# Fetching five of 202 edge pairs' source rows one row at a time from the SP and ACT queues

## The chip, the cores and the metric

One NeuronCore of a Trainium2 chip runs the whole kernel. The metric is device time in microseconds of one execution; lower is better. Three executions of the kernel before took 2658.31, 2687.99 and 2688.67 us, a median of 2687.99 us. The profiled execution took 2666.05 us.

## The reference

The kernel computes one message-passing layer of a graph network with 6250 nodes, 206250 edges (both directions of 100000 drawn edges plus a loop per node, sorted by destination) and 128 features, all in float32.

```python
h = maximum(layernorm(x), 0)
W   = silu(edge_attr @ fw1 + fb1) @ fw2 + fb2          # [206250, 128], a filter per edge
xn  = silu(h @ aw1 + ab1) @ aw2 + ab2                  # [6250, 128], a row per node
msg = W * xn[src]                                      # gather of source rows
agg = segment_sum(msg, dst, 6250)
out = x + h + silu(agg @ ow1 + ob1) @ ow2 + ob2
```

The gather `xn[src]` picks 206250 rows of 512 bytes in random order. How these rows come into on-chip memory is what the change is about.

## The kernel before

**Tiling.** The edges are cut into 202 pairs (`PAIRS`), each of 8 tiles (`L`) of 128 edges, so one pair needs 1024 rows of `xn`. Turn s of the main loop handles pair s. A start-up part computes `xn` for all nodes in seven chunks and writes it to the DRAM tensor `node_table`; SP issues these writes (L379) and then writes the residual (L386). After that SP has nothing to do until the end of the kernel, apart from reading the count of left-over edges (L359).

**Where a pair's rows come from.** There are three sources.
- 184 *main* pairs: POOL issues one indirect DMA per tile (L439), eight per pair (four for the last), into `xg`, which has room for three pairs (`XG`). Before pair i's gathers POOL waits on `msg_done` of the main pair three before it (L436), that is, until DVE has multiplied those rows.
- 6 *early* pairs at turns 36, 51, 66, 81, 96, 111: their input rows are gathered during the start-up into `e_x`, and the node network runs on them turn by turn. `e_x` keeps one pair in each of six slots; slot r is free once turn `EARLY_TURNS[r]` has multiplied its rows.
- 12 *selected* pairs at turns 26, 41, 56, ..., 191: PE fetches their rows from the on-chip copy `parts` by multiplying with one-hot columns (L1133), six or seven blocks times three matmuls in each of turns 10 to 189. They stand in `sel_rows`.

**What a turn does.** PE multiplies the filters of pair s (L1022 and L1090), then runs a job of the side networks if one is due, then the hidden layer of pair s + 2 (L1077, which signals `pe_turn`), then the sums of an earlier pair (L1142), then the selection (L1133). ACT evaluates the job's result and the hidden layer of pair s + 2 (L504). DVE makes the one-hots (L816, L818, L861), multiplies the filters with the rows (L826, which signals `msg_done`), sums them (L829), masks them (L833) and sums again. All orders are written out at build time; there is no scheduler at run time. The job's result and the hidden layer share one PSUM bank, so PE's L1077 of a turn with a job waits until ACT has taken the job's result.

**Edge features.** ACT issues the loads of `attr` (L542), four turns' worth at a time (`PART`), into one of two halves of the tile.

**Issue points the change touches.** In `pair` of the scalar block (L592) ACT does, in order: transfers, the job, `silu_hid(s + 2)`, the copy of a finished selection (L605), then `pieces`. A wait on ACT or SP holds everything behind it in that engine's program.

Of the kernel before, what the change touches and what calls it, by code (L numbers as in the profile page):

```python
# [5 lines left out]
P = 128  # L6
# [11 lines left out]
EDGE_TILES = PAIRS * L  # L18
XG = 3
SETS = 4  # L20
PART = 4
EARLY_PAIRS = 6
EPS = 1e-5

# [45 lines left out]
assert max(SEL_TURNS) < PAIRS - 3  # L70


PIECES = [(i, min(8, NODE_TILES - i)) for i in range(0, NODE_TILES, 8)]
assert len(PIECES) + 2 < SEL_FROM


EARLY_TURNS = tuple(SEL_TURNS[r] + SEL_STEP // 2 + 3 for r in range(EARLY_PAIRS))
MAIN_TURNS = [s for s in range(PAIRS) if s not in EARLY_TURNS + SEL_TURNS]
assert len(MAIN_TURNS) == PAIRS - len(EARLY_TURNS + SEL_TURNS)
MAIN_OF = {s: i for i, s in enumerate(MAIN_TURNS)}  # L80
EARLY_OF = {s: i for i, s in enumerate(EARLY_TURNS)}

# [119 lines left out]
def run(c, d=0):  # L202

    return c + (1 + AHEAD - d)
# [4 lines left out]
    return run(s + FILL)  # L209


def gnn_layer(nc, x, e_src_t, src_t, sel_src_t, dst_t, attr_t, node_wts_t, wts_t, cols_t, rows_t, out):
# [3 lines left out]
    table = nc.dram_tensor("node_table", [NODE_TILES * P, F], f32).ap()  # L216
    resid = nc.dram_tensor("residual", [NODE_TILES * P, F], f32).ap()

    def node_rows(t, first, n):
# [5 lines left out]
    with ExitStack() as ctx:  # L225
# [3 lines left out]
        def sem(name):  # L229
# [43 lines left out]
        onehot = sb("onehot", [P, OH_SETS, 2, WIN])  # L273


        e_x = sb("e_x", [P, EARLY_PAIRS * L, F])
        e_moments = sb("e_moments", [P, 4, EARLY_PAIRS * L])
        warm = sb("warm", [P, 1])
# [6 lines left out]
        part_of = sb("part_of", [P, 2])  # L285
        sel_T = hT[:, GC:2 * GC]


        spare = sb("spare", [P, max(3 * EDGE_TILES // 2 + 4 * PAIRS, SEL_MOST * GC)])
        sel_hot = spare[:, 0:SEL_MOST * GC].bitcast(bf16).rearrange("p (b k e) -> p b k e", b=2, k=SEL_MOST)  # L290
# [45 lines left out]
        attr_in = [sem("attr_in_a"), sem("attr_in_b")]  # L336
        gathered = [sem(f"gathered{s}") for s in range(XG)]
        half_gathered = [sem(f"half_gathered{i}") for i in range(2 * len(HALVED))]
        e_gathered = [sem(f"e_gathered{r}") for r in range(EARLY_PAIRS)]
        pe_turn, hid_done, oh_done, msg_done, masked, first_done, red_done, half_msg, half_first, half_masked, half_red, win_done, group_done = (  # L340
            sem(n) for n in ("pe_turn", "hid_done", "oh_done", "msg_done", "masked", "first_done", "red_done", "half_msg",
# [11 lines left out]
            sem(n) for n in ("r_din", "r_key", "r_in", "r_gat", "r_l1", "r_hid", "r_fil", "r_msg", "r_one", "r_win",  # L353
                             "r_add", "r_taken"))
        a_l1, a_mid, a_l2, a_res, a_out = (sem(n) for n in ("a_l1", "a_mid", "a_l2", "a_res", "a_out"))

        def edges_left(eng):
            eng.wait_ge(s_left, 1)
# [4 lines left out]
        @block.sync  # L363
        def _(sp):
            sp.dma_start(e_src[:, :], e_src_t).then_inc(e_src_in, 16)
            for c in range(N_CHUNKS):
                for first, g, n in transfers(c):
                    sp.dma_start(xs[:, first:first + g * n, :].rearrange("p (g t) f -> p g t f", g=g), chunk_rows(x, first, g, n))\
                        .then_inc(s_x[c], 16)
            sp.dma_start(dst_i, dst_t).then_inc(s_dst, 16)  # L370
            sp.dma_start(wts[:, :, :], wts_t).then_inc(s_wts, 16)
            sp.dma_start(src[:, :], src_t).then_inc(src_in, 16)

            sp.sem_inc(s_tab, 16 * AHEAD)
# [36 lines left out]
        def _(pool):  # L411
# [17 lines left out]
            pool.wait_ge(src_in, 16)  # L429
            pool.wait_ge(s_tab, 16 * (AHEAD + table_writes(N_CHUNKS - 1)))  # L430

            for i, s in enumerate(MAIN_TURNS):


                if i >= XG:
# [17 lines left out]
        def _(act):  # L453
# [128 lines left out]
            def pieces(s):  # L582
# [4 lines left out]
                if 0 <= s - 1 < len(PIECES):  # L587
                    first, n = PIECES[s - 1]
                    act.wait_ge(stage_in[(s - 1) % 2], ((s - 1) // 2 + 1) * 16)
                    act.copy(parts[:, 0, first:first + n, :], hs[:, (s - 1) % 2, 0:n, :]).then_inc(part_hi, 1)  # L590

            def pair(s):  # L592
                transfers_of(s)
                for a in range(FILL) if s == 0 else ():
# [5 lines left out]
                if s in SEL_LAST:  # L600
                    h = SEL_LAST[s]
                    act.wait_ge(sel_summed, h + 1)
                    if h >= 1:
                        act.wait_ge(job_taken, job_done(("turned", h - 1)))
                    act.copy(sel_T, sel_ps).then_inc(sel_copied, 1)  # L605
                pieces(s)
                if s == STD_TURN:
                    act.wait_ge(s_var, 3)
# [36 lines left out]
        def _(dve):  # L645
# [251 lines left out]
            def pair(s):  # L897
# [11 lines left out]
                if s in EARLY_OF:  # L909
                    r = EARLY_OF[s]  # L910
                    rows_of = e_x[:, r * L:(r + 1) * L, :]
                    dve.wait_ge(job_taken, job_done(("second", 2 * r + 1)))
                elif s in SEL_OF:
                    rows_of = sel_rows[:, :, :]
                    dve.wait_ge(job_taken, job_done(("turned", 2 * SEL_OF[s] + 1)))
# [342 lines left out]
```

## Time and profile before

| | us |
|---|---|
| three executions | 2658.31, 2687.99, 2688.67 |
| profiled execution | 2666.05 |
| its span, first to last instruction | 2664.0 |
| PE busy | 1967.9 (74%) |
| DVE busy | 1480.9 (56%) |
| POOL busy | 1440.4 (54%) |
| ACT busy | 359.9 (14%) |
| mean granted TensorE clock | 0.824 |

A row of the profile's group list gives the source line, the engine, the operation, output and input by name, the count, the busy time, the mean duration, and the time that the engine sat idle before these instructions with what ended it. "Releaser remote" means that the profile could not name the instruction that ended a wait. DMA issues do not count as busy; they stand under the queue names SPq, ACTq and POOLq. A matmul's start is recorded and its end is modelled. Times of a timeline are microseconds from the start of the span.

### The profile page before, as it was taken

How to read it: one execution, taken by the hardware profiler on the slowest of the kernel's cores; microseconds unless marked ns; L12 is line 12 of the kernel's file. 1: busy time of each engine (PE TensorE's matmuls, PEld its weight loads, DVE VectorE, ACT ScalarE, POOL GpSimd, SP SyncE). 2: the span in 40 equal slices, each digit the busy share in tenths (PEclk: the TensorE clock that was granted, in tenths of full speed). 3: DMA queues.
4: the chain of work that ended last, by engine and by line, in shares of the span. 5: the costliest groups of instructions: out<-in, count | busy, mean ns of one | idle time of the engine just before them, and what ended most of it. 6: DMA issues, size and time to landing. Idle time of an engine off the chain costs nothing.

```text
span 2664.0 us, 24312 instructions
## 1 busy us (share of the span) xinstructions
PE 1967.9 (74%) x9385; PEld 1145.3 (43%) x9385; DVE 1480.9 (56%) x2778; ACT 359.9 (14%) x442; POOL 1440.4 (54%) x1523
## 2 busy tenths in 40 slices
PE   3455767777788776788878788778778788787755
PEld 2243434444444444444444344435444444444433
DVE  5376455555555555566556565645555565465545
ACT  3221111111111111111101011111010111011011
POOL 5465555454454544545655654555555556555553
PEclk9766878888888988988888888878778888797876
DMA  4432221121122222212222222222212222222221
GB/s 139 155 104 72 59 60 55 53 77 55 52 64 68 62 58 64 63 57 80 62 58 72 60 76 59 60 62 76 58 58 73 63 60 79 64 61 71 61 60 48
DMA packets 76661, 181.82 MB, mean 68 GB/s; under 512 B 26816, under 2 KB 37184, under 8 KB 70144
## 3 DMA queue, kind: packets, MB, share of 16 engines
q0 software_dynamic: 48512, 99.45, 14.2%
q10 hardware_dynamic: 21648, 69.22, 7.7%
q1 hardware_dynamic: 6384, 11.58, 1.2%
q8 instruction: 75, 1.23, 0.2%
q14 instruction: 42, 0.34, 0.0%
HBM read 170.50 MB, written 9.63 MB: 68 GB/s over the span
## 4 chain that ended last, share of the span: by engine, by line
PE 56%; another core or an unknown queue 24%; issue 13%; DVE 3%; ACT 3%; DMA 0%; ACTq 0%; SPq 0%; DVEq 0%
PE banks L1133 27%; PE banks L1090 11%; PE banks L1077 9%; PE banks L1142 4%; PE banks L1022 3%; ACT hid L504 1%; DVE sums L829 1%; PE banks L1029 1%; DVE banks L833 0%; PE banks L1018 0%; DVE banks L826 0%; PE banks L1119 0%; PE banks L1013 0%; ACT hs L578 0%
## 5 line engine op out<-in xcount | busy, mean ns | idle before, releaser
L439 POOL DMA_INDIRECT xg<-node_table,src x1468 | 1393.5, 949 | 1163.2 <-DVE banks L826 724.5
L1133 PE MATMUL banks<-spare,parts 128*128 128x512 bf16 x3528 | 921.7, 412 | 117.8 <-issue 113.5
L861 DVE TENSOR_SCALAR spare<-sel_marks 128x512 bf16<-128x512 bf16 x1176 | 265.8, 295 | 826.1 <-PE banks L1077 412.5
L1133 PEld LDWEIGHTS banks<-spare,parts 128*128 128x128 bf16 x3528 | 367.0, 106 | 607.0 <-issue 302.3
L1090 PE MATMUL banks<-wts,hid 128*128 128x128 f32 x3224 | 500.1, 297 | 111.4 <-issue 110.4
L1090 PEld LDWEIGHTS banks<-wts,hid 128*128 128x128 f32 x3224 | 486.9, 213 | 176.2 <-issue 139.8
L1077 PE MATMUL banks<-attr,wts 50*128 50x512 f32 x806 | 278.9, 765 | 302.5 <-issue 79.2
L829 DVE TENSOR_REDUCE sums<-banks 128x128 f32<-128x1024 f32 (+1 forms) x408 | 493.9, 1211 | 13.6
L504 ACT ACTIVATE hid<-banks,cols 128x1024 f32<-128x1024 f32 x202 | 224.8, 1113 | 1418.9 <-remote 914.9
L826 DVE TENSOR_TENSOR banks<-banks,xg 128x1024 f32<-128x1024 f32 (+1 forms) x186 | 224.5, 1207 | 88.5 <-remote 86.1
L833 DVE TENSOR_TENSOR banks<-banks,other 128x1024 f32<-128x1024 f32 (+1 forms) x204 | 248.7, 1219 | 7.0
L1077 PEld LDWEIGHTS banks<-attr,wts 50*128 50x128 f32 x806 | 73.6, 217 | 341.2 <-issue 281.4
L1022 PE MATMUL banks<-bias_rows,ones_b 128*128 128x512 bf16 x429 | 178.6, 416 | 35.4 <-issue 20.0
L1142 PEld LDWEIGHTS banks<-onehot,sums 128*128 128x128 f32 x816 | 128.0, 223 | 175.9 <-issue 168.5
L1142 PE MATMUL banks<-onehot,sums 128*128 128x88 f32 x816 | 157.9, 326 | 14.5 <-issue 8.3
L850 DVE TENSOR_SCALAR sel_hi<-sel_src 128x512 bf16<-128x512 uint8 x24 | 10.3, 429 | 163.0 <-remote 106.5
L1022 PEld LDWEIGHTS banks<-bias_rows,ones_b 128*128 128x128 bf16 x429 | 46.3, 108 | 75.7 <-issue 38.4
L818 DVE SCALAR_TENSOR_TENSOR onehot<-iota,ends,onehot 128x88 f32<-128x88 f32 x202 | 62.7, 311 | 9.6 <-remote 2.4
L427 POOL DMA_INDIRECT e_x<-in_x,e_src x48 | 45.7, 952 | 35.0 <-DVE res L726 18.8
L816 DVE TENSOR_SCALAR onehot<-iota,ends 128x88 f32<-128x88 f32 x202 | 53.7, 266 | 0.1
L1018 PE MATMUL banks<-node_wts,mid 128*128 128x128 f32 x194 | 26.7, 288 | 16.8 <-ACT mid L478 15.2
L1007 PE MATMUL banks<-ident,hs 128*128 128x128 f32 x97 | 16.6, 308 | 25.2 <-ACT hs L471 22.6
(109 smaller groups left out, 485.0 us busy)
## 6 DMA issues: line engine op xcount, KB each, us to landing
attr<-in_attr ACTq DMA_DIRECT2D x50, 1024.0 KB
xg<-node_table,src POOLq DMA_INDIRECT x1468
sel_src<-in_sel_src ACTq DMA_DIRECT2D x24, 256.0 KB
hs<-node_table ACTq DMA_DIRECT2D x6, 512.0 KB
resid_s<-residual ACTq DMA_DIRECT2D x8, 256.0 KB
out<-res ACTq DMA_DIRECT2D x8, 256.0 KB
parts<-in_x SPq DMA_DIRECT2D x3, 512.0 KB, 6.0
node_table<-res SPq DMA_DIRECT2D x3, 512.0 KB
```

Of the source, the lines that this page charges most:

```text
L439: pool.indirect_dma_start(xg[:, i % XG, j, :], None, table[:, :], bass.IndirectOffsetOnAxis(ap=src[:, s * L + j:s * L + j + 1], axis=0))\
L504: act.activation(hid[:, s % 2, 0:n], hid_ps[:, 0:n], ACT.Silu, bias=cols[:, 0:1]).then_inc(hid_done, 1)
L818: dve.scalar_tensor_tensor(out=to[:, 1, :], in0=nodes, scalar=ends[:, 1, s:s + 1], in1=to[:, 0, :], op0=ALU.is_equal, op1=ALU.subtract).th ...
L826: dve.tensor_tensor(to, to, rows_of, ALU.mult).then_inc(signal, 1)
L829: return dve.reduce_sum(sums[:, at, m, :], of.rearrange("p j f -> p f j"), AX.X)
L833: dve.tensor_tensor(to, to, other[:, t:t + n].rearrange("p (j o) -> p j o", o=1).to_broadcast([P, n, F]), ALU.mult).then_inc(signal, 1)
L861: last = dve.tensor_scalar(sel_hot[:, s % 2, i, :], sel_marks[:, k % 2, :], float(k // 2 + 1), None, ALU.is_equal)
L1022: pe.matmul(to[:, 0:n_tiles * P], ones_b[:, :], bias_rows[:, kind, 0:n_tiles, :].rearrange("p j f -> p (j f)"), start=True, stop=False)
L1077: i = pe.matmul(hid_ps[:, GC * half:GC * half + GC], fw1_s[at, :], attr[at, cols_of], start=True, stop=True)
L1090: i = pe.matmul(to[:, j * P:(j + 1) * P], hid[:, s % 2, at], w["fw2_s"][:, :], start=False, stop=j == TPG - 1)
L1133: step = pe.matmul(sel_ps, parts[:, m, k, :], sel_hot[:, s % 2, i, :], start=k == 0 and m == 0, stop=last)
L1142: i = pe.matmul(sum_ps[:, to:to + WIN], sums[:, at, m, :], onehot[:, s % OH_SETS, m, :], start=False, stop=stop and m == 1)
```

## The change

Five main pairs, those of turns 54, 104, 152, 196 and 198, no longer go through POOL. Their rows are fetched one by one: 1024 direct DMAs of 512 bytes each per pair. The host passes their source indices in a new input `row_src`, DVE multiplies them by 512 once (byte offsets into `node_table`), and the issuing engine loads 32 of them at a time into registers.
- SP does this for the first four pairs, 4096 rows, one after another, behind the start-up writes. The first pair goes into a new tile `row_first`. The next three go into slots 1, 2 and 3 of `e_x`, each after a wait until turn 51, 66 or 81 has used that slot.
- ACT does it for the fifth pair, into slot 0 of `e_x`: in turns 37 to 196 it issues six or seven rows at the end of each turn, behind `silu_hid` and the selection's copy, and in every fifth turn it first loads 32 offsets.
- DVE waits for four semaphores per such pair before it multiplies.
- POOL's main pairs are 179 instead of 184.
- To make room for `row_first`, `PART` falls from 4 to 3: a load of `attr` covers three turns.

```diff
-PART = 4
+PART = 3
+ROW_TURNS = (54, 104, 152, 196, 198)
+ROW_TILES = (L, L, L, L, L)
+ROW_SLOTS = (None, 1, 2, 3, 0)
+ROWS_AT_ONCE = 32
+ROW_SIGNALS = 4
+ROW_BYTES = 4 * F
+ACT_ROWS = ROW_PAIRS - 1
+ACT_ROWS_FROM = 37
+ACT_ROWS_TURNS = 160
+ACT_ROWS_STEPS = 5
-MAIN_TURNS = [s for s in range(PAIRS) if s not in EARLY_TURNS + SEL_TURNS]
+MAIN_TURNS = [s for s in range(PAIRS) if s not in EARLY_TURNS + SEL_TURNS + ROW_TURNS]
...
+        def begins_of(eng, m, q):
+            _, begins = nc.values_load_multi_w_load_instructions(
+                row_src[q:q + 1, m * ROWS_AT_ONCE:(m + 1) * ROWS_AT_ONCE], engines=[eng.engine], ...)
+            return begins
+        def row_transfer(eng, m, q, i, begin):
+            p, j = divmod(q * ROWS_AT_ONCE + i, ROW_TILES[m])
+            eng.dma_start(row_x(m)[p:p + 1, j, :].bitcast(u8), table_bytes[:, bass.ds(begin, ROW_BYTES)])\
+                .then_inc(row_in[m][q % ROW_SIGNALS], 16)
...
# SP
+            sp.dma_start(row_src, row_src_t).then_inc(row_src_in, 16)
...
+            sp.wait_ge(row_scaled, 1)
+            for m in range(ROW_PAIRS - 1):
+                if ROW_SLOTS[m] is not None:
+                    sp.wait_ge(msg_done, run(EARLY_TURNS[ROW_SLOTS[m]]))
+                for q in range(ROW_TILES[m] * P // ROWS_AT_ONCE):
+                    begins = begins_of(sp, m, q)
+                    for i, begin in enumerate(begins):
+                        row_transfer(sp, m, q, i, begin)
...
# ACT, behind silu_hid and the selection's copy in pair(s)
+            def rows_by_act(s):
+                t = s - ACT_ROWS_FROM
+                if not 0 <= t < ACT_ROWS_TURNS:
+                    return
+                q, k = divmod(t, ACT_ROWS_STEPS)
+                if t == 0:
+                    act.wait_ge(row_scaled, 1)
+                    act.wait_ge(msg_done, run(EARLY_TURNS[ROW_SLOTS[ACT_ROWS]]))
+                if k == 0:
+                    begins[:] = begins_of(act, ACT_ROWS, q)
+                for i in range(k * ROWS_AT_ONCE // ACT_ROWS_STEPS, (k + 1) * ROWS_AT_ONCE // ACT_ROWS_STEPS):
+                    row_transfer(act, ACT_ROWS, q, i, begins[i])
...
# DVE
+            dve.wait_ge(row_src_in, 16)
+            dve.tensor_scalar(row_src, row_src, float(ROW_BYTES), None, ALU.mult).then_inc(row_scaled, 1)
...
+                elif s in ROW_OF:
+                    m = ROW_OF[s]
+                    rows_of = row_x(m)
+                    for landed in row_in[m]:
+                        dve.wait_ge(landed, 16 * ROW_TILES[m] * P // ROW_SIGNALS)
```

## Rows read from the trace of the kernel before

**Rows 1.** The page: the engines' busy time, and slices of the span.

```profile
PE 1967.9 (74%) x9385; PEld 1145.3 (43%) x9385; DVE 1480.9 (56%) x2778; ACT 359.9 (14%) x442; POOL 1440.4 (54%) x1523
POOL 5465555454454544545655654555555556555553
```

**Rows 2.** Waits, whole span: engine, line, releaser: us in total, times, longest.

```profile
ACT hid L504 <- remote: 914.9, 68, 21.4
POOL xg L439 <- DVE banks L826: 724.5, 97, 19.5
POOL xg L439 <- issue: 424.0, 1370, 1.7
DVE banks L826 <- remote: 97.3, 11, 21.2
```

**Rows 3.** Timeline of POOL, 1318 to 1346 us: start, us, instruction, idle before.

```profile
1318.51 0.94 POOL L439 DMA_INDIRECT xg<-node_table,src  x1 [7.78 <-DVE banks L826]
1319.76 0.94 POOL L439 DMA_INDIRECT xg<-node_table,src  x1 [0.31 <-issue]
...
1337.31 0.94 POOL L439 DMA_INDIRECT xg<-node_table,src  x1 [0.30 <-issue]
1344.03 0.94 POOL L439 DMA_INDIRECT xg<-node_table,src  x1 [5.78 <-DVE banks L826]
```

**Rows 4.** Groups of PE in two stretches: 1304.2 to 1313.5, then 1320.7 to 1325.5 us.

```profile
L1133 PE MATMUL banks<-spare,parts 128*128 128x512 bf16 x9 | 4.3, 495 | 4.6 <-issue 4.3
...
L1133 PE MATMUL banks<-spare,parts 128*128 128x512 bf16 x21 | 4.7, 379 | 0.0
```

**Rows 5.** Timeline of DVE: the multiplications of turns 26, 71, 116 and 191.

```profile
471.54 1.23 DVE L826 TENSOR_TENSOR banks<-banks,sel_rows 128x1024 f32<-128x1024 f32 x1
...
1060.20 1.23 DVE L826 TENSOR_TENSOR banks<-banks,sel_rows 128x1024 f32<-128x1024 f32 x1
...
1606.10 1.22 DVE L826 TENSOR_TENSOR banks<-banks,sel_rows 128x1024 f32<-128x1024 f32 x1
...
2557.29 1.23 DVE L826 TENSOR_TENSOR banks<-banks,sel_rows 128x1024 f32<-128x1024 f32 x1 [11.20 <-remote]
```

**Rows 6.** Timeline of SP's queue, start-up: start, us for the issues together, instruction.

```profile
6.88 0.44 SPq L370 DMA_DIRECT2D spare<-in_dst  x1
7.37 0.43 SPq L371 DMA_DIRECT2D wts<-in_wts  x1
7.84 0.49 SPq L372 DMA_DIRECT2D src<-in_src  x1
...
95.04 8.09 SPq L386 DMA_DIRECT2D residual<-parts  x9
```

**Rows 7.** The register load of line 359 and the issue of line 542: min/median/max ns.

```profile
L359 SPq TENSOR_LOAD <-n_left x1: 467/467/467, 109.0 to 109.0; - x1
...
L542 ACTq DMA_DIRECT2D attr<-in_attr x49: 334/335/1307, 171.6 to 2598.0; - x49
```

**Rows 8.** Timeline of DVE: the multiplications of turns 51, 54, 104 and 196.

```profile
802.28 1.22 DVE L826 TENSOR_TENSOR banks<-banks,e_x 128x1024 f32<-128x1024 f32 x1
...
839.54 1.22 DVE L826 TENSOR_TENSOR banks<-banks,xg 128x1024 f32<-128x1024 f32 x1
...
1457.36 1.22 DVE L826 TENSOR_TENSOR banks<-banks,xg 128x1024 f32<-128x1024 f32 x1
...
2603.41 1.23 DVE L826 TENSOR_TENSOR banks<-banks,xg 128x1024 f32<-128x1024 f32 x1
```

**Rows 9.** Timeline: ACT's hidden layer, PE's next filters; then two issues of ACT.

```profile
1320.35 1.11 ACT L504 ACTIVATE hid<-banks,cols 128x1024 f32<-128x1024 f32 x1 [1.59 <-PE banks L1077]
...
1325.28 0.38 PE L1022 MATMUL banks<-bias_rows,ones_b 128*128 128x512 bf16 x1
...
1345.77 0.33 ACTq L554 DMA_DIRECT2D sel_src<-in_sel_src  x1
1346.15 0.44 ACTq L542 DMA_DIRECT2D attr<-in_attr  x1
```

More of the change, by code:

```diff
@@ L70 @@
 assert max(SEL_TURNS) < PAIRS - 3
+ROW_TURNS = (54, 104, 152, 196, 198)
+ROW_TILES = (L, L, L, L, L)
+ROW_SLOTS = (None, 1, 2, 3, 0)
+ROW_OF = {s: m for m, s in enumerate(ROW_TURNS)}
+ROW_PAIRS = len(ROW_TURNS)
+ROWS_AT_ONCE = 32
[5 more added lines that the diff above has]
+ACT_ROWS_STEPS = 5
 PIECES = [(i, min(8, NODE_TILES - i)) for i in range(0, NODE_TILES, 8)]
@@ L77 @@
 EARLY_TURNS = tuple(SEL_TURNS[r] + SEL_STEP // 2 + 3 for r in range(EARLY_PAIRS))
-MAIN_TURNS = [s for s in range(PAIRS) if s not in EARLY_TURNS + SEL_TURNS]
-assert len(MAIN_TURNS) == PAIRS - len(EARLY_TURNS + SEL_TURNS)
+MAIN_TURNS = [s for s in range(PAIRS) if s not in EARLY_TURNS + SEL_TURNS + ROW_TURNS]
+assert len(MAIN_TURNS) == PAIRS - len(EARLY_TURNS + SEL_TURNS + ROW_TURNS)
 MAIN_OF = {s: i for i, s in enumerate(MAIN_TURNS)}
@@ L209, in after, with gnn_layer @@
     return run(s + FILL)
-def gnn_layer(nc, x, e_src_t, src_t, sel_src_t, dst_t, attr_t, node_wts_t, wts_t, cols_t, rows_t, out):
+def gnn_layer(nc, x, e_src_t, src_t, sel_src_t, row_src_t, dst_t, attr_t, node_wts_t, wts_t, cols_t, rows_t, out):
     f32, i32, bf16, u8 = mybir.dt.float32, mybir.dt.int32, mybir.dt.bfloat16, mybir.dt.uint8
@@ L216, in gnn_layer @@
     table = nc.dram_tensor("node_table", [NODE_TILES * P, F], f32).ap()
+    table_bytes = table.bitcast(u8).rearrange("(o n) b -> o (n b)", o=1)
     resid = nc.dram_tensor("residual", [NODE_TILES * P, F], f32).ap()
@@ L273, in gnn_layer @@
         onehot = sb("onehot", [P, OH_SETS, 2, WIN])
+        row_src = moments.rearrange("p m t -> p (m t)")[0:L * P // ROWS_AT_ONCE, 0:ROW_PAIRS * ROWS_AT_ONCE].bitcast(i32)
+        row_first = sb("row_first", [P, L, F])
         e_x = sb("e_x", [P, EARLY_PAIRS * L, F])
@@ L286, in gnn_layer, with row_x @@
         sel_T = hT[:, GC:2 * GC]
+        def row_x(m):
+            return row_first[:, :, :] if ROW_SLOTS[m] is None else e_x[:, ROW_SLOTS[m] * L:(ROW_SLOTS[m] + 1) * L, :]
         spare = sb("spare", [P, max(3 * EDGE_TILES // 2 + 4 * PAIRS, SEL_MOST * GC)])
@@ L338, in gnn_layer @@
         half_gathered = [sem(f"half_gathered{i}") for i in range(2 * len(HALVED))]
+        row_rest = sem("row_rest")
+        row_src_in, row_scaled = sem("row_src_in"), sem("row_scaled")
+        row_in = [[sem(f"row_in{m}_{i}") for i in range(ROW_SIGNALS)] for m in range(ROW_PAIRS)]
         e_gathered = [sem(f"e_gathered{r}") for r in range(EARLY_PAIRS)]
@@ L355, in gnn_layer @@
         a_l1, a_mid, a_l2, a_res, a_out = (sem(n) for n in ("a_l1", "a_mid", "a_l2", "a_res", "a_out"))
+        def begins_of(eng, m, q):
+            _, begins = nc.values_load_multi_w_load_instructions(
+                row_src[q:q + 1, m * ROWS_AT_ONCE:(m + 1) * ROWS_AT_ONCE], engines=[eng.engine], min_val=0, max_val=(NODE_TILES * P - 1) * ROW_BYTES,
+                skip_runtime_bounds_check_because="a source index is one of a node")
+            return begins
+        def row_transfer(eng, m, q, i, begin):
+            p, j = divmod(q * ROWS_AT_ONCE + i, ROW_TILES[m])
+            eng.dma_start(row_x(m)[p:p + 1, j, :].bitcast(u8), table_bytes[:, bass.ds(begin, ROW_BYTES)]).then_inc(row_in[m][q % ROW_SIGNALS], 16)
         def edges_left(eng):
@@ L430, in _, with rest_of_rows @@
             pool.wait_ge(s_tab, 16 * (AHEAD + table_writes(N_CHUNKS - 1)))
+            def rest_of_rows(m):
+                pool.wait_ge(msg_done, run(EARLY_TURNS[ROW_SLOTS[m]]))
+                for j in range(ROW_TILES[m], L):
+                    pool.indirect_dma_start(row_x(m)[:, j, :], None, table[:, :],
+                                            bass.IndirectOffsetOnAxis(ap=src[:, ROW_TURNS[m] * L + j:ROW_TURNS[m] * L + j + 1], axis=0))\
+                        .then_inc(row_rest, 16)
             for i, s in enumerate(MAIN_TURNS):
+                for m, r in enumerate(ROW_TURNS):
+                    if ROW_TILES[m] < L and MAIN_TURNS[i - 1] < r < s:
+                        rest_of_rows(m)
                 if i >= XG:
@@ L590, in pieces @@
                     act.copy(parts[:, 0, first:first + n, :], hs[:, (s - 1) % 2, 0:n, :]).then_inc(part_hi, 1)
+            def rows_by_act(s):
[10 more added lines that the diff above has]
+                    row_transfer(act, ACT_ROWS, q, i, begins[i])
+            begins = [None] * ROWS_AT_ONCE
             def pair(s):
@@ L605, in pair @@
                     act.copy(sel_T, sel_ps).then_inc(sel_copied, 1)
+                rows_by_act(s)
                 pieces(s)
@@ L912, in pair @@
                     dve.wait_ge(job_taken, job_done(("second", 2 * r + 1)))
+                elif s in ROW_OF:
[3 more added lines that the diff above has]
+                        dve.wait_ge(landed, 16 * ROW_TILES[m] * P // ROW_SIGNALS)
+                    if ROW_TILES[m] < L:
+                        dve.wait_ge(row_rest, 16 * sum(L - n for n in ROW_TILES[:m + 1]))
                 elif s in SEL_OF:
@@ L1234 @@
     attr[:, :NG] = features.reshape(PAIRS, P, 2, TPG, NG).transpose(2, 4, 0, 3, 1).reshape(2, NG, PAIRS * GC)
+    row_src = np.zeros((L * P // ROWS_AT_ONCE, ROW_PAIRS, ROWS_AT_ONCE), src_p.dtype)
+    for m, s in enumerate(ROW_TURNS):
+        nodes = src_p[s, :, :ROW_TILES[m]].reshape(-1, ROWS_AT_ONCE)
+        row_src[:len(nodes), m] = nodes
+    row_src = row_src.reshape(-1, ROW_PAIRS * ROWS_AT_ONCE)
     arrays = {
@@ L1239 @@
         "sel_src": np.ascontiguousarray(src_p[list(SEL_TURNS)].reshape(SEL_PAIRS, P, 2, TPG).transpose(0, 2, 3, 1).reshape(SEL_HALVES, GC)),
+        "row_src": row_src,
         "dst": np.ascontiguousarray(dst_p.transpose(1, 0, 2).reshape(P, EDGE_TILES)),
```

## The prediction

> **What bounds the kernel now.** The page comes first. No engine is full: PE is busy 74% of the span, DVE 56%, POOL 54%, and POOL's slices stay at four to six tenths from start to end [rows 1]. So I read the waits next. POOL's 724.5 us of waiting for DVE's multiplication is a wait for a free buffer, so its gathers are mostly ahead of their users; DVE waits for something it cannot name only 97.3 us in 11 cases, which bounds from above what late gathers cost directly. Between its indirect DMAs POOL loses another 424.0 us, 0.3 us each [rows 2].
>
> The timeline shows the rhythm behind these averages. POOL issues 16 gathers in a row, one every 1.25 us, then stands idle 5.78 us until a multiplication frees a buffer: two pairs in 1344.03 - 1318.51 = 25.5 us, 12.8 us a pair [rows 3]. PE does not run evenly under that. In the stretch before such a run it starts 9 selection matmuls in 9.3 us, with half the time in idle that no wait explains, and in the next stretch 21 in 4.7 us [rows 4]. The slow stretch falls late in a run of POOL's, and PE is fast again about three microseconds after its last gather. What makes PE slow there the trace does not name. What it does show is that two main turns take 25.5 us, of which 20 are POOL's own sequence, although neither POOL nor PE would need that much. I therefore treat POOL's main pairs as what sets the time, without claiming that POOL is full.
>
> **The change, part by part.**
>
> *Forty gathers leave POOL.* Five pairs times 8 gathers times 1.25 us is 50 us of POOL's sequence [rows 3]. What a pair off POOL is worth in turns I read between selected pairs, which are 15 turns apart. From turn 71 to 116 the three periods have 13 main pairs each and take (1606.10 - 1060.20) / 3 = 182.0 us. From turn 116 to 191 the five periods have 14 and take (2557.29 - 1606.10) / 5 = 190.2 us [rows 5]. The difference, 8.2 us, is my value for each of the pairs of turns 54, 104 and 152: 24.6 us. The ends: nothing, if the neighbours take up the time, and 12.8 us, if a whole share of POOL's cycle goes [rows 3]. Turns 196 and 198 lie behind the selection, where PE has the least to do and POOL's 10 us a pair are the nearest row: 20 us. Together 44.6 us, ends 0 and 64.
>
> *4096 rows on SP.* SP is otherwise idle, so they cost nothing as long as they land in time. The price of one row: issues behind each other on SP start 0.47 us apart in the start-up's small ones and 8.09 / 9 = 0.90 us apart where large transfers are in flight [rows 6]; a lone issue on ACT takes 0.33 us, a register load 0.467 us [rows 7]. The trace does not show how many registers one load fills. With one load per row that is up to 0.47 + 0.47 = 0.94 us, with none in sight 0.33 us. A row issue has one line to describe instead of 128, so I take 0.42 us plus a quarter of a load, 0.12 us: 0.54 us. The ends for the range are 0.33 and 0.94.
>
> When they must be there: the first pair from the end of the start-up (109 us) to turn 54 at 839.5 us, 0.71 us a row. The later three can't start before turn 51 has freed the slot at 802.3 us, and the last of their 3072 rows is needed at turn 196, at 2603.4 us now and about 2563 us if 40 us are won: 0.586 and 0.573 us a row. Turn 104 asks for (1457.4 - 802.3) / 1024 = 0.64 us [rows 7, 8]. At 0.54 us SP is done at 802.3 + 1659 = 2461 us. So the step is hidden, by SP's idle time, with 6% to spare; if that cover goes, turn 196 waits, see the rivals.
>
> *1024 rows on ACT.* Each turn gains 6.4 issues at about 0.44 us, 2.8 us, and every fifth the loads of 32 offsets, 8 x 0.47 = 3.7 us [rows 7, 9]. They stand behind the hidden layer and ahead of the next turn's job, on whose result PE waits. From ACT's start on the hidden layer to PE's next filters are 4.9 us [rows 9]; the filters' first half and the job put about 1.8 us more before PE needs ACT, 6.7 us in all. The ordinary turn (1.1 + 2.8 = 3.9 us) fits. The turn with loads (7.6 us) is 0.9 us late, 32 times, if nothing else is waited for: 29 us at most. Since a pair of turns is as long as POOL's run in most places, I charge 5 us. The ends are 0 and 29 us, or far more if a load fills one register: 32 x 0.47 = 15 us in each of these 32 turns.
>
> *The rest.* DVE gets one operation on a small tile and twenty waits, under 1 us. `attr` comes in 68 loads instead of 51, each 0.33 us of ACT's queue [rows 7] in 14% of whose time ACT works [rows 1]: nothing, and 17 x 0.44 = 7 us if ACT's cover goes. The load of `row_src` goes ahead of SP's residual writes, one more issue of 0.5 us [rows 6] during the preparation of the destinations: nothing.
>
> Sum: 44.6 - 5 - 1 = about 39 us, so 2666 - 39 = 2627 us for an execution like the profiled one. That one is 22 us below the median of the three runs; two of them lie at 2688, one at 2658. I put the median of the changed kernel between 2627 and 2649 and say 2640 us.
>
> **The rivals.**
>
> *A whole share of the cycle.* Each pair off POOL takes 12.8 us with it and ACT costs nothing: 2666 - 64 = 2602 us. For it: the 25.5 us rhythm. Against it: the periods of 13 and 14 pairs differ by less, and the turn itself still needs PE's and DVE's 7 us.
>
> *Nothing gained.* The freed POOL time goes into its waits, of which it has 724.5 us already, or ACT's 29 us eat most of the rest: 2666 to 2690 us. For it: the three periods of 13 pairs from turn 26 to 71, when the node network's jobs are on, take (1060.20 - 471.5) / 3 = 196.2 us, more than those with 14 [rows 5].
>
> *SP too slow.* The mechanism is in one place: DVE's wait at turn 196 for the fourth pair's last row. It decides from 0.573 us a row on. With the start-up's spacing of 0.50 us and a quarter load, 0.62 us, the last row lands at 802.3 + 3072 x 0.62 = 2707 us, and from turn 196 to the end are 2664 - 2603 = 61 us, less 10 for the lighter last turns: a span of 2758, so 2760 us. At the ends it is brutal: 0.90 us a row give 3570 + 51 = 3620 us. For it: the longest spacings seen are far over the limit, and a register address may cost extra. Against it: those long spacings stand beside 512 KB transfers, here each issue moves half a KB.
> The Trainium skill (DMA: Bandwidth & Descriptors, section Latency and other measured facts) puts the floor of a register load at about 600 ns and says that the compiler unrolls it by four; the one load on SP took 467 ns [rows 7], so the trace has it shorter. By the page a row would be an estimated 0.50 + 0.15 = 0.65 us and the kernel an estimated 2850 us.
> The same page (section Rules for kernel authors) wants small transfers coalesced, since under 64 KB one pays mostly overhead. The trace agrees on the price: a gather moves 128 rows in 1.25 us of its queue, SP's issues would need some 70 us for as many. It says nothing on whether an idle queue makes that free.
>
> *More traffic, longer slow stretches.* PE's slow stretches come with a busy POOL queue. If the steady stream of small issues on SP brings them on sooner, say 2 us more in each of some 75 rhythms (2600 / 25.5, less those at turns off POOL), the kernel takes 150 us more than the forecast, about 2790 us. Nothing in the trace shows SP issuing beside the main loop, so only the likeness of the two queues speaks for it.
>
> **How the numbers follow.** The forecast has 45%, the whole share 15%, nothing gained 16%, SP too slow 17%, longer stretches 7%. The likeliest case alone spans 2610 to 2665 us. The range runs from 2585, below the whole share, to 2765 us, so that it takes in the mildest lateness of SP; left out are the 7%, half of the late cases, and a little at the bottom. A measurement of this kernel tells about 2% from no change, which puts the borders at 2634 and 2742 us against the median of 2688. Faster by more: half of the forecast's share and the whole-share case, 37%. Slower by more: both late cases, 24%. Within: the remaining 39%.
>
> **What would show it.** SP's issues in the main loop 0.50 to 0.57 us apart, loads included, and a gap before turn 51. POOL with 1428 gathers and the same 1.25 us between them. No idle time of DVE before the multiplications of turns 54, 104, 152, 196 and 198. The periods from turn 41 to 56, 101 to 116 and 146 to 161 each some 8 us shorter, the others unchanged, and the stretch from turn 191 to the end some 20 us shorter. ACT's idle time before L504 falling by its issues and no new wait of PE for ACT. I am wrong if DVE idles at turn 196, if ordinary periods without such a pair get longer, or if the five turns simply take the time that their gathers took.

## The result, and the profile after

| | before | after |
|---|---|---|
| median of the runs, us | 2681.58 (2658.31 to 2688.67, 4 runs) | 2868.57 (2853.53 to 2870.83, 4 runs) |
| span of the profiled execution, us | 2664.0 | 2868.9 |

The ratio is 1.070, 95% interval 1.062 to 1.078: the changed kernel is 7% slower, 188 us by the ratio. Forecast were 2640 us and a range up to 2765. Here and below a ratio leaves out executions more than 1.5% above the fastest one of the same kernel, while the medians named are over all of them, so the two can differ a little.

First the page of the kernel after: busy time, POOL's slices, and the chain that ended last, by engine and by line.

```profile
PE 1951.0 (68%) x9208; PEld 1146.3 (40%) x9385; DVE 1477.5 (52%) x2779; ACT 360.8 (13%) x442; POOL 1403.2 (49%) x1483
...
POOL 5565454544444444554555545545553455455520
...
SPq 44%; issue 28%; another core or an unknown queue 12%; PE 9%; DVE 4%; ACT 2%; ACTq 1%; DMA 0%; DVEq 0%
```

Apart from POOL's forty gathers, busy times are nearly those of [rows 1]; what has grown is the time between them. SP's queue, which had no part in the loop before, now stands at the head of the chain. The waits of the whole span (engine, line, releaser: us in total, times, longest):

```profile
ACT hid L554 <- remote: 1007.4, 78, 22.5
POOL xg L489 <- DVE banks L894: 982.3, 120, 88.6
...
POOL xg L489 <- issue: 406.8, 1307, 3.1
...
DVE banks L894 <- DMA e_x<-node_table: 108.6, 2, 91.9
```

POOL waits 258 us more for a free buffer than in [rows 2], so POOL has become less the limit, not more. New is the last line: DVE waits for fetched rows. The timeline of DVE's multiplications shows where. They are those of turns 26, 71, 116, 152, 191 and 196.

```profile
485.58 1.22 DVE L894 TENSOR_TENSOR banks<-banks,sel_rows 128x1024 f32<-128x1024 f32 x1
...
1105.76 1.22 DVE L894 TENSOR_TENSOR banks<-banks,sel_rows 128x1024 f32<-128x1024 f32 x1
...
1677.98 1.22 DVE L894 TENSOR_TENSOR banks<-banks,sel_rows 128x1024 f32<-128x1024 f32 x1
...
2176.80 1.23 DVE L894 TENSOR_TENSOR banks<-banks,e_x 128x1024 f32<-128x1024 f32 x1 [16.69 <-DMA e_x<-node_table]
...
2692.63 1.23 DVE L894 TENSOR_TENSOR banks<-banks,sel_rows 128x1024 f32<-128x1024 f32 x1 [0.38 <-PE banks L1152]
...
2827.34 1.23 DVE L894 TENSOR_TENSOR banks<-banks,e_x 128x1024 f32<-128x1024 f32 x1 [91.88 <-DMA e_x<-node_table]
```

Against [rows 5, 8] turn 26 is 14 us late, turn 71 46 us, turn 116 72 us, turn 191 135 us and turn 196 224 us; at the end 205 us are left. So there are two losses. One is spread over the turns, unevenly: 135 us by turn 191, although the relief of POOL should have won time there. The other is a single wait of 91.88 us at turn 196, the place that the prediction's third rival named.

The line that issues the rows (duration min/median/max in ns, first and last start), and the line that loads 32 offsets into registers:

```profile
L388 SPq DMA_DIRECT2D e_x<-node_table x3072: 2/228/1410, 841.1 to 2826.0; - x192
...
L388 SPq DMA_DIRECT2D row_first<-node_table x1024: 2/228/1385, 108.0 to 797.0; - x171
```

```profile
L381 SPq TENSOR_LOAD <-moments x128: 5/2158/2641, 105.8 to 2813.7; - x128
```

The three pairs in `e_x` took (2826.0 - 841.1) / 3071 = 0.646 us a row, above the limit of 0.573 that the prediction had worked out for being in time at turn 196. Yet the median issue took only 0.228 us and a load of 32 offsets 2.16 us, 0.07 us a row. The missing time is in certain stretches. The timeline of SP's queue, which merges a stretch of such issues into one line (start, us, count), once for 1305.5 to 1315.4 us and once for 1320 to 1334 us, and then PE in the second stretch:

```profile
1305.51 10.06 SPq L388 DMA_DIRECT2D e_x<-node_table  x24
```

```profile
1319.93 12.85 SPq L388 DMA_DIRECT2D e_x<-node_table  x7
```

```profile
1328.60 0.27 PE L1165 MATMUL banks<-wts,hid 128*128 128x128 f32 x1 [1.87 <-issue]
1331.41 0.37 PE L1165 MATMUL banks<-wts,hid 128*128 128x128 f32 x1 [2.55 <-issue]
1334.21 0.37 PE L1165 MATMUL banks<-wts,hid 128*128 128x128 f32 x1 [2.43 <-issue]
1335.64 0.37 PE L1165 MATMUL banks<-wts,hid 128*128 128x128 f32 x1 [1.06 <-issue]
```

24 rows in 10 us, then 7 in 12.9, while POOL gathers from 1315.44 to 1335.2 us. The slow stretches of [rows 4] hit SP too. PE is slower in this one than before, and falls back some 10 us into POOL's run, not some 14 us as in the run of [rows 3]. It then starts a matmul of 0.37 us only every 1.4 to 2.8 us, all of the time between put down to issue (time in which an engine waits for nothing that the profile shows).

### The profile page after: what moved, and what is told of

It reads as the page before. It is cut to its first block, busy times and chain, and to the rows that moved or that the text cites. A ratio compares the mean times of both kernels' runs of the same rounds, so it can differ in the third digit from the quotient of the medians.

```text
span 2868.9 us, 34535 instructions
## 1 busy us (share of the span) xinstructions
PE 1951.0 (68%) x9208; PEld 1146.3 (40%) x9385; DVE 1477.5 (52%) x2779; ACT 360.8 (13%) x442; POOL 1403.2 (49%) x1483
## 4 chain that ended last, share of the span: by engine, by line
SPq 44%; issue 28%; another core or an unknown queue 12%; PE 9%; DVE 4%; ACT 2%; ACTq 1%; DMA 0%; DVEq 0%
SPq L388 38%; SPq L381 6%; PE banks L1208 3%; PE banks L1152 2%; PE banks L1165 2%; DVE sums L897 1%; DVE banks L894 1%; DVE banks L901 1%; PE banks L1217 1%; ACTq L388 0%; PE banks L1093 0%; ACT hs L628 0%; PE banks L1097 0%; ACT hid L554 0%
## 5 line engine op out<-in xcount | busy, mean ns | idle before, releaser
L489 POOL DMA_INDIRECT xg<-node_table,src x1428 | 1355.8, 949 | 1398.9 <-DVE banks L894 982.3
L1208 PE MATMUL banks<-spare,parts 128*128 128x512 bf16 x3386 | 899.8, 415 | 120.3 <-issue 113.0
L1208 PEld LDWEIGHTS banks<-spare,parts 128*128 128x128 bf16 x3528 | 375.4, 108 | 595.5 <-issue 289.3
L1165 PE MATMUL banks<-wts,hid 128*128 128x128 f32 x3224 | 483.1, 290 | 147.9 <-issue 146.5
L1165 PEld LDWEIGHTS banks<-wts,hid 128*128 128x128 f32 x3224 | 469.2, 206 | 192.2 <-issue 156.1
L1152 PE MATMUL banks<-attr,wts 50*128 50x512 f32 x806 | 299.9, 778 | 357.3 <-issue 90.5
L894 DVE TENSOR_TENSOR banks<-banks,xg 128x1024 f32<-128x1024 f32 (+2 forms) x181 | 218.5, 1207 | 74.4 <-remote 58.2
L1097 PE MATMUL banks<-bias_rows,ones_b 128*128 128x512 bf16 x394 | 157.0, 398 | 110.4 <-DVE sums L897 97.2
L894 DVE TENSOR_TENSOR banks<-banks,e_x 128x1024 f32<-128x1024 f32 x10 | 12.2, 1223 | 108.6 <-DMA e_x<-node_table 108.6
L1194 PE MATMUL banks<-ident,hT 128*128 128x128 f32 x96 | 16.9, 305 | 49.7 <-ACT hT L670 36.6
```

Source lines behind the costliest of these rows:

```text
L894: dve.tensor_tensor(to, to, rows_of, ALU.mult).then_inc(signal, 1)
L1097: pe.matmul(to[:, 0:n_tiles * P], ones_b[:, :], bias_rows[:, kind, 0:n_tiles, :].rearrange("p j f -> p (j f)"), start=True, stop=False)
L1152: i = pe.matmul(hid_ps[:, GC * half:GC * half + GC], fw1_s[at, :], attr[at, cols_of], start=True, stop=True)
L1165: i = pe.matmul(to[:, j * P:(j + 1) * P], hid[:, s % 2, at], w["fw2_s"][:, :], start=False, stop=j == TPG - 1)
L1208: step = pe.matmul(sel_ps, parts[:, m, k, :], sel_hot[:, s % 2, i, :], start=k == 0 and m == 0, stop=last)
```

## The experiments

Theory T: the slow stretches are a shared slowness of issuing. SP's additional instructions take part in it, lengthen it for PE, and are themselves held up until they are late. Rivals: the loss comes from the other edits (R1), from ACT's rows (R2), or from the waits for late rows alone (R3). The kernels of each set below ran on one chip together with the kernel before; the five sets ran on five chips. The kernel before took about 2690, 2640 and 2650 us on three of them and 1938 us on the other two, so every ratio is against the kernel before on the same chip, and I name its time each time.

**Which part costs (kernel before: 2688 us).** The rows not fetched at all. The five pairs multiply rows gathered for other pairs, so their part of the output is left out.

```
-                for m in range(ROW_PAIRS - 1): ...   # SP's stream
-                rows_by_act(s)
-                    for landed in row_in[m]: dve.wait_ge(landed, ...)
```

> The kernel after without its 5120 row transfers and their register loads, on SP and on ACT; the five pairs multiply rows that were gathered earlier for other pairs, so they wait for nothing, and POOL still makes 1428 gathers. Theory A (the rows' own instructions or transfers lengthen the ordinary turns, and their lateness the end): nothing is left of the loss and the relief of POOL shows, 2610 to 2640 us. Rival B (the loss up to turn 191 comes from what else changed: attribute blocks of three pairs and the changed order of POOL's gathers): 2700 to 2760 us. My step of 44.6 us for the 40 gathers is right if it is near 2630, and worthless if it is near 2670.

2644 us, ratio 0.988 (0.981 to 0.996): 32 us faster, between 11 and 52. The forecast of 44.6 us for the 40 gathers lies inside that interval, and R1 falls: the other edits together with the relief still win time. The relief also shows where it was forecast. In this execution the period from turn 41 to 56 is 10.9 us shorter than in the profile before, that from 146 to 161 10.1 us and the end from turn 191 on 17 us; that from 101 to 116 is unchanged. Periods without such a pair scatter by up to 5 us, so this is a hint and no measurement.

Then the pairs by their fetchers:

```
-ROW_TURNS = (54, 104, 152, 196, 198)
+ROW_TURNS = (54, 104, 152, 198,)          # first
+ROW_TURNS = (198,)                        # second: ACT's pair alone
+ROW_TURNS = (54, 104, 152, 196,)          # third: SP's pairs alone
-                rows_by_act(s)            # third
```

> Turn 196 goes back to POOL: SP fetches three pairs instead of four, ACT still one. Theory: SP's lateness at turn 196 is worth 89 us of the loss and the longer ordinary turns 135. SP ends its third pair by 2180 us, so the kernel takes 2868 - 89 - (turns 140 to 191 after SP stopped run at the old periods: some 35) + 10 for the eight gathers = 2755 us. If lateness were the whole loss, it would be near 2680; if it cost nothing because the end had its own limit, near 2860.

> Only ACT's pair (turn 198) is fetched by rows; the other four stay with POOL, SP issues no rows. If SP's stream is what lengthens the ordinary turns: 2665 to 2700 us, ACT's part costing little. If ACT's six or seven rows at the end of 160 turns and its 32 register loads of 2.2 us are the cause: the 135 us remain and it is near 2800.

> Only SP's four pairs are fetched by rows; turn 198 goes back to POOL, ACT issues no rows. If SP's stream is the cause: 2840 to 2870 us, as the kernel after. If ACT's rows are: 2868 - 135 = 2730 us. If each has its share, in between, and with the result for ACT alone the two shares add up to the loss.

Without turn 196's pair: 2774 us, ratio 1.035 (1.027 to 1.043), 94 us over the kernel before. ACT alone: 2700 us, 1.012 (1.006 to 1.018), 32 us over. SP alone: 2854 us, 1.066 (1.058 to 1.075), 178 us over. The pair of turn 196 costs 188 - 94 = 94 us, its own eight gathers saved already taken off. Not all of that is waiting: without this pair SP stops issuing at 2167 us instead of 2826. The wait at turn 196 alone was 91.9, 74.9 and 91.1 us in the three traces of the kernel after. ACT's part is dearer than the 5 us I charged: 32 us (16 to 48), and by the forecast's value some 8 more for the pair it relieved. Beside SP's stream it hardly shows (1.070 against 1.066, intervals overlapping), so the shares don't add up. R2 falls: SP's stream alone gives nearly the whole loss.

**The stream without a user.** POOL gathers all pairs again and ACT fetches no rows; SP fetches three pairs' rows that nobody reads, once with addresses from registers and once with fixed ones (rows five apart instead of random ones). With them, attribute blocks of three pairs alone, and a wait on POOL for the landing of each pair's gathers.

```
-MAIN_TURNS = [s for s in range(PAIRS) if s not in EARLY_TURNS + SEL_TURNS + ROW_TURNS]
+MAIN_TURNS = [s for s in range(PAIRS) if s not in EARLY_TURNS + SEL_TURNS]
-            for m in range(ROW_PAIRS - 1):
+            for m in range(ROW_PAIRS - 2):
-                    begins = begins_of(sp, m, q)                      # fixed addresses only
+                    begins = [ROW_BYTES * (5 * (q * 32 + i) + 11) ...]
```

```
-PART = 4
+PART = 3
```

```
                 if i >= XG:
                     pool.wait_ge(msg_done, run(MAIN_TURNS[i - XG]))
+                    if s not in HALVED:
+                        pool.wait_ge(gathered[(i - 1) % XG], ((i - 1) // XG + 1) * 16 * L)
```

> The kernel before with attribute blocks of three pairs instead of four, nothing else. My step charged this at nothing, at most 7 us: 2688 to 2695 us. If the rise of attr issues and their waits matters to the turns, above 2705 us.

> All main pairs are gathered by POOL as before, ACT issues no rows, and SP fetches the rows of three pairs (3072) that nobody reads or waits for. Theory A (the stream itself lengthens the turns, whoever uses it): with three SP pairs and ACT's the time was 2774 against 2644 without rows; less 9 for the eight gathers of turn 196 and about 20 for ACT that leaves 100 us, so 2690 + 100 = 2790 us. Rival B (turns that wait for their rows are what costs: turns 54, 104, 152): 2690 to 2700 us.

> As the kernel with the unused stream, but the 3072 transfers have fixed addresses: no register loads and no register moves on SP, the same number of transfers of the same size to the same places. If the transfers or their issue are the cost: 2790 us again. If the register loads (96 of 2.2 us) or the doubled number of SP instructions are: 2690 to 2740 us.

> The kernel before, where POOL waits after each main pair until its eight gathers have landed, so that it never issues more than eight in a row. Theory of the slow stretches (PE falls to one matmul per 0.70 us some 12 to 14 us into an unbroken run of gathers, and stays there until the run ends): the runs of 16 are broken, the slow stretches go, and the turns shorten towards 8 gathers x 1.25 + 2 us = 12.0 us instead of 12.75: 2688 - 0.75 x 150 = 2575 us. Rival (POOL is simply the bound and the waits are added to it): 2 us x 150 pairs less the 2.7 us a turn of idle it has now, so 2690 to 2990 us.

The wait on POOL is an edit of the kernel before, as are the blocks of three. This set ran on a chip where the kernel before takes 1937.5 us, 28% less. Blocks of three: 1.000 (0.999 to 1.001). The stream: 1.000 (0.999 to 1.001). Fixed addresses: 1.000. The landing waits: 1.240 (1.238 to 1.242). The page of the kernel with the unused stream (busy, chain, granted clock in tenths) shows another regime:

```profile
PE 1712.6 (88%) x9208; PEld 1062.6 (55%) x9385; DVE 1498.5 (77%) x2779; ACT 360.7 (19%) x442; POOL 1453.2 (75%) x1523
...
PEclk9778999999999999999999999999999999999876
...
POOL 59%; issue 19%; PE 17%; DVE 2%; DMA 1%; ACT 0%; POOLq 0%; SPq 0%; ACTq 0%; DVEq 0%
```

Here POOL really is the chain: its gathers run without a break, and 3072 additional issues on SP disturb nobody. SP's line there:

```profile
L388 SPq DMA_DIRECT2D e_x<-node_table x2048: 227/228/640, 572.3 to 1390.5; - x187
```

(1390.5 - 572.3) / 2047 = 0.400 us a row, loads included, and no issue over 0.64 us. That is the undisturbed price; with fixed addresses it was 0.300 us.

The same kernels again, with the kernel after itself (kernel before now: 2639 us):

> The kernel after once more, since calls can land on chips that run the kernel before in 2690 us (with slow stretches) or in 1937 us (without). On a chip with slow stretches: 2870 us, 180 above the kernel before. On one without: there POOL's gathers are the chain, 40 fewer of them take 8.8 us off each of five turns, and SP, at 0.40 to 0.48 us a row in the run with the unused stream there, ends its last pair at 565 + 3072 x 0.43 = 1886 us, about when turn 196 is due: 1895 to 1920 us, 1 to 2% faster. If the change were bad by itself, whatever the chip, 7% slower in both.

> SP fetches the rows of three pairs that nobody reads; POOL gathers all. On a chip with slow stretches: if the stream itself lengthens the turns, 2690 + 100 = 2790 us; if only late rows cost, 2690 to 2700 us. On a chip without them: 1937 us again.

> As the kernel with the unused stream, with fixed addresses: no register loads, no register moves, the same 3072 transfers. On a chip with slow stretches: 2790 us if the transfers or their issue are the cost, 2690 to 2740 us if the register loads and the doubled number of SP instructions are. Without slow stretches: 1937 us.

> The kernel before with POOL waiting after each main pair until its gathers have landed. Without slow stretches it cost 2.5 us for each of 183 pairs (2403 against 1937 us). On a chip with slow stretches: if they need a long unbroken run of gathers, breaking the runs makes them go and the time falls towards the same 2400 us, 10% faster; if they come from something else, the waits only add: 2690 to 2990 us.

The kernel after: 2833 us, 1.080 (1.072 to 1.087). The unused stream: 2747 us, 1.044 (1.038 to 1.051), 117 us for rows that nobody waits for, so R3 falls as the whole story. Its trace shows the slow stretches sooner: over all runs of POOL's of 15 us and more between 600 and 2000 us, PE's first idle of over 0.7 us put down to issue came 11.0 us into the run (median), with fixed addresses 11.7 us and in the kernel after 10.4 us, against 14.8 us in the kernel before and 13.5 us without rows. With fixed addresses: 2704 us, 1.026 (1.016 to 1.035), 67 us for the same 3072 transfers with half of SP's instructions (no move per row, no load per 32). So leaving out the register work takes away about four tenths of the stream's cost. That may be the work itself or the time that it takes: without it SP needs 0.396 us a row here instead of 0.652 and is through at 1626 us instead of 2176. What is left is due to the issues or their transfers, which these runs don't separate.

PE beside the unused stream, from 1325 us, and in the kernel without rows, from 1305 us, both late in a run of POOL's:

```profile
1325.86 0.35 PE L1167 MATMUL banks<-wts,hid 128*128 128x128 f32 x1 [1.40 <-issue]
1327.26 0.37 PE L1167 MATMUL banks<-wts,hid 128*128 128x128 f32 x1 [1.04 <-issue]
1328.68 0.37 PE L1167 MATMUL banks<-wts,hid 128*128 128x128 f32 x1 [1.05 <-issue]
1330.78 0.60 PE L1167 MATMUL banks<-wts,hid 128*128 128x128 f32 x2 [1.73 <-issue]
```

```profile
1305.48 0.58 PE L1155 MATMUL banks<-wts,hid 128*128 128x128 f32 x1 [1.06 <-issue]
1306.91 0.37 PE L1155 MATMUL banks<-wts,hid 128*128 128x128 f32 x1 [0.84 <-issue]
1307.61 0.37 PE L1155 MATMUL banks<-wts,hid 128*128 128x128 f32 x1 [0.33 <-issue]
1308.31 0.59 PE L1155 MATMUL banks<-wts,hid 128*128 128x128 f32 x2 [0.33 <-issue]
```

Without the stream the matmuls are down to 0.70 us apart; with it the spacings are 1.4 us and more, multiples of the same 0.70. In the stretch 1324.4 to 1336.4 us SP issued 8 rows (11.92 us in its timeline), with their moves 16 instructions, again about one per 0.70 us. Two engines share a slow issue there. That is a reading of two stretches. That the mechanism is a shared one is argued from it and not shown; that the cost falls to six tenths with half of the instructions fits it.

The landing waits are the surprise: 2390 us, 0.910 (0.905 to 0.916), 9% faster than the kernel before, and nearly the same time as on the other chip (2403 us). POOL's timeline and its waits in this kernel:

```profile
1303.51 0.95 POOL L441 DMA_INDIRECT xg<-node_table,src  x1 [0.31 <-issue]
1306.84 0.94 POOL L441 DMA_INDIRECT xg<-node_table,src  x1 [2.38 <-DMA xg<-node_table,src]
...
1315.66 0.94 POOL L441 DMA_INDIRECT xg<-node_table,src  x1 [0.30 <-issue]
1318.87 0.94 POOL L441 DMA_INDIRECT xg<-node_table,src  x1 [2.27 <-DMA xg<-node_table,src]
```

A pair every 12.0 us with a pause of 3.3 us from issue to issue, no run of 16 and no wait for DVE (one of 5.1 us in the whole span). Against [rows 3] the pause costs POOL 2 us a pair and takes the slow stretches away. The waits of the whole span say so too. Here is the time that PE's weight loads (PEld) stood idle by "issue", added up over all lines, in the profiled executions:

| kernel | kernel before on that chip, us | PEld idle by issue, us |
|---|---|---|
| before | 2682 | 1018 |
| no rows | 2688 | 1031 |
| ACT's rows alone | 2688 | 1078 |
| unused stream, fixed addresses | 2639 | 1109 |
| unused stream | 2639 | 1142 |
| after | 2682, 2639, 2650 | 1136, 1107, 1126 |
| landing waits | 2639 | 345 |
| landing waits | 1938 | 248 |
| blocks of three | 1938 | 218 |
| unused stream | 1938 | 221 |

Every row stream adds to it on the one kind of chip and nothing on the other, and the landing waits remove two thirds of it. So the kernel before, too, loses its time in the slow stretches. The granted TensorE clock is no rival for the difference between the chips: it was 0.82 to 0.83 against 0.96 in the kernel before, but 0.89 to 0.90 on both with the landing waits, so it does not go with the chip.

**How long a pause, and does the change pay then?** Here the question was what the stream does where POOL pauses.

```
+        last_in = [sem(f"last_in{s}") for s in range(XG)]      # the eighth gather signals here
+                        pool.wait_ge(gathered[(i - 1) % XG], ((i - 1) // XG + 1) * 16 * 7)
+                    if s not in HALVED and i % 2 == 0:             # after every second pair, all eight
```

> The kernel after, with POOL waiting after each main pair until its gathers have landed. If the row stream costs time only through the slow stretches, these are gone with POOL's long runs, SP takes 0.41 us a row and is done by about 1930 us, and the relief shows: five turns less of 8 x 1.25 + 2.5 = 12.5 us each, 2390 - 62 = 2330 us. If the stream costs 100 us whatever PE's pace: 2430 us and more.

> The kernel before with POOL waiting after each main pair for the landing of its first seven gathers only, so the pause is about 1.2 us shorter. If a pause of any kind breaks the slow stretches: 2390 - 1.25 x 180 = 2165 us. If the shorter pause is not enough, the slow stretches come back: between 2390 and 2640 us. On a chip without them: 1937 + 180 x 0.75 to 1.25 = 2070 to 2165 us.

> The kernel after with the same shorter wait for seven of eight gathers. Where the kernel before with it takes 2165 us and the stream costs nothing outside slow stretches, five turns less of 11.3 us: 2110 us, the fastest of all on a chip with slow stretches. If the shorter pause leaves slow stretches, the stream makes them longer and it is slower than the kernel before with the same wait.

> The kernel before with POOL waiting for the landing after every second main pair, so that runs of 16 gathers remain and end in a pause. If it is the length of the run that brings the slow stretch (PE falls to one matmul per 0.70 us 13 us into a run): they stay, 2600 to 2700 us. If any regular pause is enough: 2390 - 2.5 x 90 = 2165 us.

Again a chip without slow stretches (kernel before: 1938 us), so all pauses only cost. The kernel after with landing waits: 2320 us, 1.197 (1.195 to 1.199), against 1.240 for the kernel before with the same waits on the other chip without slow stretches: the change wins 4.3 points, 83 us, where 62 were expected. With the wait for seven of eight: 2117 us, 1.094 (1.092 to 1.096), without the change and 2101 us, 1.085 (1.082 to 1.088), with it: 16 us won, where 56 were expected. Some of the rest is in POOL's waits for landings, 204.2 us in 176 cases without the change and 232.1 us in 172 with it. The wait after every second pair: 2139 us, 1.103. Where issuing is not slow the change does what it was made for. The kernel after itself was not seen on such a chip.

The last two (kernel before: 2650 us):

> The kernel after once more. On a chip with slow stretches: 7 to 8% slower than the kernel before, as twice already. On one without (kernel before 1938 us): the unused stream cost nothing there and POOL's chain gets 5 x 8.8 us shorter: 1895 to 1920 us, if SP is in time for turn 196.

> The kernel after with POOL waiting for seven of each pair's eight gathers to land. On a chip with slow stretches: if the pause of 2 us keeps PE and SP out of them and the stream costs nothing otherwise, 2100 us as on the chip without, 20% faster than the kernel before there; if it is too short, PE falls to one matmul per 0.70 us or less in some turns and the time is 2200 to 2600 us. On a chip without: 2101 us again.

The kernel after: 2819 us, 1.061 (1.055 to 1.067), so it is 6 to 8% slower in all three measurements. With the shorter pause: 2756 us, 1.042 (1.034 to 1.050), still slower than the kernel before. The slow stretches are there; PE, with POOL in a run that began at 1310.38 us:

```profile
1322.63 0.33 PE L1221 MATMUL banks<-onehot,sums 128*128 128x88 f32 x1 [0.48 <-issue]
1324.02 0.31 PE L1221 MATMUL banks<-onehot,sums 128*128 128x88 f32 x1 [1.07 <-issue]
1324.75 0.30 PE L1221 MATMUL banks<-onehot,sums 128*128 128x88 f32 x1 [0.42 <-issue]
```

and POOL's queue at the border between two pairs there:

```profile
1321.30 0.95 POOL L492 DMA_INDIRECT xg<-node_table,src  x1 [1.14 <-DMA xg<-node_table,src]
```

With idle times of 1.14 us and the row stream the slowness stayed; with 2.3 us and no row stream it went. Which of the two differences decides is open, since the shorter wait without the stream did not run on a chip with slow stretches. It also seldom made a pause: POOL waited for a landing 44 times, 58.9 us in all, and otherwise for DVE. The landing wait without the row stream is the one complete version that beat the kernel before clearly on a chip of the kind of the forecast's profile; on the other kind the kernel before is the fastest seen. The kernel after with the full landing wait was not run on a chip with slow stretches.

## Why the prediction was wrong

*What bounds the kernel.* I called the slow stretches unnamed and took POOL's main pairs as the setter. On chips without them that would have been right (10 us a pair, POOL without a break). On this one PE and SP wait for issuing: a POOL that paused more was 9% faster. The reading of [rows 3, 4] saw the pattern and passed over it.

*Forty gathers leave POOL.* Not contradicted: 1428 gathers at 949 ns, 1.25 us apart; 44.6 us forecast, 32 (11 to 52) measured, with the other edits in it.

*4096 rows on SP.* This is the step that failed, in its sentence "so the step is hidden, by SP's idle time". My price of a row was too high, not too low: 0.54 us against 0.400 undisturbed. At that price the deadline of 0.573 would have been kept easily. What broke it was that SP joined the slow stretches, 0.646 us a row with them, and started 39 us later because turn 51 came later. The step was charged nothing; the runs show 117 us for three pairs that nobody uses and 94 us for the fourth. The Trainium skill (DMA: Bandwidth & Descriptors, section Latency and other measured facts) puts the floor of a register load at about 600 ns; a load of 32 offsets took 2.16 us here, 0.07 us a row. The estimate of 0.65 us a row and 2850 us that I had made from that page came close by luck: undisturbed a row took 0.400 us, and the rest was the slow stretches.

*Hidden at no cost.* The unused stream cost 117 us. A queue's idle time was no cover here: on this kind of chip its instructions held up PE's.

*1024 rows on ACT.* 5 us charged, ends 0 and 29; about 40 without SP's stream, hardly anything beside it. One load filled all 32 registers in 2.2 us, where I had counted eight loads and 3.7 us, so the turn's 7.6 us were an overestimate, and still the cost was larger. ACT's rows seem to draw on the same thing: with them alone PE's weight loads stood idle by issue 1078 us, against 1031 without rows. No run separated that from PE's waits for ACT.

*The rest.* Nothing for the blocks of three, measured by themselves only on a chip without slow stretches.

*The rivals.* Both late cases came true at once, the fourth in the way it was told, as slow stretches that come sooner. I had them as alternatives with 17 and 7 in 100; but a longer slow stretch is exactly what makes SP late. Their measured terms, 117 and 94 us, less the relief of 32, give 179 of the 188 us, and ACT's part the rest. The terms come from different chips, each with an interval of some 20 us to either side, so that this closes so well is partly luck. The range ended at 2765 us because it held only one of them, and of that one only the mildest lateness.

## What to carry to other kernels

An idle queue is not free space until a run shows it: issue the planned stream without a user and time that first. An unexplained slow phase in the profile deserves the first experiment, before anything is moved past it; here one added wait on POOL was worth more than the whole change could have been. Two failure cases with a common cause belong in one case with their sum. And a verdict can depend on the chip: the stream that cost 4% on one cost nothing on another, and the wait that won 9% on the first cost 24% there.

## What the runs showed of the hardware

- The same kernel took 1938 us on two chips and 2640 to 2690 us on the others, steady within 0.3% and 3%. The difference is in stretches late in POOL's runs of indirect DMAs, in which PE starts a matmul with its weight load every 0.70 us or at a multiple of it, be it 128x88, 128x128 or 128x512, and SP about one instruction in that time. In the kernel before they ended some 3 us after POOL's last gather. With 3.3 us from the last issue of a pair to the first of the next they stayed away. What differs between the chips is open.
- Away from slow stretches one row of 512 B costs 0.40 us of SP's queue with an address from a register and 0.30 us with a fixed one. The first is made of an issue of 0.23 us, a move of 0.03 us, the gaps between them, and 2.2 us for each load of 32 values.
- What is shared stays open. The Trainium skill (NOTIFIC — the notification-queue block, section Overflow: three behaviours, one of which stalls the engine) says that the block which writes the instructions' records holds up its producers when its internal buffers are full; that would hit several engines at once, as here. No run here shows that it is this. Each execution in the record comes with a granted clock and so may have been recorded; whether the slow stretches exist without the recording is open too.
